# Decay tables of two chunked recurrences: ScalarE with a per-head bias in place of a bf16 matmul

## The reference, cut to what matters

```python
G = jnp.cumsum(gc, axis=-1)                                # layer 0: 32 heads, chunks of 128
decay = jnp.where(causal, jnp.exp(G[..., :, None] - G[..., None, :]), 0.0)
y_intra = jnp.einsum('bhnij,bhnjd->bhnid', scores * decay, xc)
...
A_cum = jnp.cumsum(A_dt, axis=-1)                          # layer 1: 128 heads, chunks of 128
L = jnp.exp(_segsum(A_dt))                                 # exp(A_cum_i - A_cum_j) for i >= j
Y_diag = jnp.einsum('bzlhn,bzshn,bhzls,bzshp->bzlhp', Cc, Bc, L, xch)
```

## Time and profile before

| | |
|---|---|
| median of 3 runs | 2715.9 us (2715.47 to 2716.67) |
| the profiled execution | 2718.86 us |
| its span in the trace | 2717.1 us |
| PE busy, share of the span | 2567.2 us, 94% |
| DVE busy | 1867.5 us, 69% |
| POOL busy | 1431.7 us, 53% |
| ACT busy | 1364.3 us, 50% |
| DMA | 118.79 MB, mean 44 GB/s |

### The profile page before, as it was taken

The page is one execution under the profiler, slowest core; times in us unless marked ns, Lnnn a source line. Parts: engine busy times, 40 slices in busy tenths (PEclk is TensorE's granted clock), DMA queues, the critical chain, the costliest instruction groups (busy, mean ns, idle before and its releaser), DMA issues.

```text
span 2717.1 us, 58923 instructions
## 1 busy us (share of the span) xinstructions
PE 2567.2 (94%) x19678; PEld 2041.7 (75%) x19678; DVE 1867.5 (69%) x2720; ACT 1364.3 (50%) x2492; POOL 1431.7 (53%) x1404
## 2 busy tenths in 40 slices
PE   4999999999999669899999999999999999999989
PEld 3778787787787448677777777777777777777777
DVE  5675766766757668767777677577676677785874
ACT  3434434334334245655664665665566646656621
POOL 1654655556546110456656656476575566574720
PEclk8999999999999869999999999999999999999999
DMA  2010110110110014211111111101111111111011
GB/s 89 24 50 27 34 44 23 44 40 19 51 36 12 17 66 138 88 33 44 40 33 58 37 38 49 38 29 52 43 38 50 33 58 34 41 49 38 18 47 47
DMA packets 72632, 118.79 MB, mean 44 GB/s; under 512 B 10310, under 2 KB 22214, under 8 KB 72373
## 3 DMA queue, kind: packets, MB, share of 16 engines
q1 hardware_dynamic: 72388, 115.61, 13.0%
HBM read 102.92 MB, written 12.65 MB: 43 GB/s over the span
## 4 chain that ended last, share of the span: by engine, by line
PE 48%; issue 4%; DVE 4%; POOL 2%; ACT 2%; DVEq 0%; POOLq 0%; ACTq 0%
PE proj L218 10%; PE proj L220 10%; PE proj L219 10%; PE core_y L1403 5%; PE core_o L1409 2%; PE turned L252 2%; DVE mx_acc L1214 2%; PE turned L1430 2%; PE decay L1462 1%; PE mx_decay L1462 1%; POOL mx_acc L1663 1%; PE mx_decay L220 1%; PE mx_decay L218 1%; PE mx_decay L219 1%; POOL mx_th L1660 1%
## 5 line engine op out<-in xcount | busy, mean ns | idle before, releaser
L201 DVE TENSOR_TENSOR slab_lo<-slab_raw,slab_hi 128x512 fp32r<-128x512 f32 (+2 forms) x272 | 256.9, 957 | 147.4 <-ACT slab_hi L192 121.6
L218 PE MATMUL proj<-slab_hi,XTL 128*128 128x512 f32 x816 | 355.0, 435 | 0.0
L218 PE MATMUL proj<-XTH,slab_lo 128*128 128x512 f32 x736 | 300.0, 408 | 37.5 <-PEq L81 14.4
L220 PE MATMUL proj<-slab_hi,XTH 128*128 128x512 f32 x816 | 320.7, 393 | 0.0
L219 PE MATMUL proj<-slab_lo,XTH 128*128 128x512 f32 x816 | 318.5, 390 | 0.0
L220 PE MATMUL proj<-XTH,slab_hi 128*128 128x512 f32 x736 | 292.3, 397 | 0.0
L219 PE MATMUL proj<-XTL,slab_hi 128*128 128x512 f32 x736 | 292.0, 397 | 0.0
L1660 POOL TENSOR_TENSOR mx_th<-mx_th,mx_acc 128x512 f32<-128x512 f32 x48 | 62.1, 1294 | 369.0 <-ACT mx_th L1560 368.9
L1677 POOL TENSOR_TENSOR mx_gate<-mx_gate,mx_hd 128x512 f32<-128x512 f32 x128 | 171.1, 1336 | 156.4 <-DVE mx_hd L1591 145.4
L218 PE MATMUL proj<-slab_hi,mx_otl 128*128 128x512 f32 x576 | 241.9, 420 | 0.0
L220 PE MATMUL proj<-slab_hi,mx_oth 128*128 128x512 f32 x576 | 227.7, 395 | 0.0
(11 more groups left out here) (351 smaller groups left out, 6719.5 us busy)
## 6 DMA issues: line engine op xcount, KB each, us to landing
slab_raw<-in_w_gate SPq DMA_DIRECT2D x64, 256.0 KB, 3.0
slab_raw<-in_w_out SPq DMA_DIRECT2D x64, 256.0 KB, 3.0
slab_raw<-in_w_x SPq DMA_DIRECT2D x60, 256.0 KB, 3.6
slab_raw<-in_w_q SPq DMA_DIRECT2D x32, 256.0 KB, 3.0
slab_raw<-in_w_g SPq DMA_DIRECT2D x32, 256.0 KB, 3.0
slab_raw<-in_w_o SPq DMA_DIRECT2D x32, 256.0 KB, 2.9
bc_scratch<-bc_acc SPq DMA_DIRECT2D x32, 256.0 KB, 2.0
slab_raw<-in_w_bc SPq DMA_DIRECT2D x20, 256.0 KB, 4.5
```

The costliest lines, as they stand in the source:

```text
L201: op = nc.vector.tensor_tensor(K.SL[par][:, c, 0:width], K.RAW[c][:, 0:width], hi, ALU.subtract)
L218: nc.tensor.matmul(to[:, 0:bh.shape[-1]], al, bh, start=(c == 0), stop=False)
L220: mm = nc.tensor.matmul(to[:, 0:bh.shape[-1]], ah, bh, start=False, stop=(c == KC - 1))
```

## The change

No decay matmul is left. `decay_phase` stores only G, in fp32, one DMA, and turns G (and R) onto the token partitions as `upto` (and `left`, negated). SP then broadcasts rows of G from DRAM to all 128 partitions: in the attention four DMAs of 512 KB a round, in the mixer eight of 512 KB a half (runs of 512 B), the first four of them ahead of everything else in the mixer's first half. ACT subtracts and clamps in one Relu a head (four of 128x128 with a bias of one column in place of one of 128x512), then takes the same Exp. Across chunks four Exps a bank, with a bias, take the place of one. The fixed rows, their buffers and their memsets are gone, and DVE now waits for the score bank by itself.

```diff
-                nc.tensor.matmul(PS[k % 2][:, :], KH[:, js], QH[:, :, qs], start=False, stop=True)
-                pe.wait_ge(S["at_rows"], HEAD + 48 * (g + 1))
-                pe.wait_ge(S["at_e"], HEAD + PAIRS * g + k - 1)
-                nc.tensor.matmul(PD[k % 2][:, :], LHS[:, int(p == 1), jt * P:(jt + 1) * P], RHS[:, b, :, (it % 2) * P:(it % 2 + 1) * P],
-                                 start=True, stop=True).then_inc(S["at_pair"], 1)
+                nc.tensor.matmul(PS[k % 2][:, :], KH[:, js], QH[:, :, qs], start=False, stop=True).then_inc(S["at_pair"], 1)
...
-            act.wait_ge(S["at_set"], HEAD + 1)
+            act.wait_ge(S["at_ld"], HEAD + 48)
...
+                            act.wait_ge(S["at_rows"], HEAD + 64 * (g + 1))
                             act.wait_ge(S["at_m"], HEAD + PAIRS * g + k - 1)
+                            alone(act)
+                            for h in range(REP0):
+                                src, head = GB[b][:, h, it * P:(it + 1) * P], ds(REP0 * g + h, 1)
+                                if p == 1:
+                                    ex = nc.scalar.activation(EX[k % 2][:, h, :], src, ACT.Exp, bias=left[:, jt, head])
+                                else:
+                                    rl = nc.scalar.activation(EX[k % 2][:, h, :], src, ACT.Relu, bias=upto[:, jt, head], scale=-1.0)
...
-            nc.vector.memset(LHS[:, :, :], 0.0)
-            nc.vector.memset(RHS[:, :, :, :], 0.0).then_inc(S["at_zero"], 1)
...
+            def row_load(q, t):
+                sp.wait_ge(S["mx_e"], HEAD + 16 * q + 2 * t - 6)
+                sp.dma_start(GB[t % 4][:, :, :], sums[ds(HH1 * q, HH1), t * P:(t + 1) * P].unsqueeze(0)
+                             .broadcast_to([P, HH1, P])).then_inc(S[f"mx_row{t % 4}"], 16)
...
+            for t in range(4):
+                row_load(0, t)
...
-                    row_loads(q, 0)
-                    row_loads(q, 1)
                     slab(q, 2)
-                    row_loads(q, 2)
-                    row_loads(q, 3)
+                    for t in range(4, NT):
+                        row_load(q, t)
...
                         slab(q, 3)
+                        for t in range(4):
+                            row_load(q + 1, t)
...
-                            nc.tensor.matmul(PD[k][:, :], LHS[b % 2][:, k, cols], RHS[b % 2][:, 4 * k:4 * k + 4, cols],
-                                             start=True, stop=True).then_inc(S["mx_d"], 1)
...
+                        act.wait_ge(S[f"mx_row{t % 4}"], HEAD + 32 * q + 16 * (t // 4 + 1))
                         for k in range(2):
-                            act.wait_ge(S["mx_d"], HEAD + 16 * q + 2 * t + k + 1)
-                            nc.scalar.activation(PD[k][:, :], PD[k][:, :], ACT.Relu, scale=-1.0).then_inc(S["mx_rl"], 1)
+                            act.wait_ge(S["mx_m"], HEAD + 16 * q + 2 * t + k - 1)
+                            if t == 0 and k == 1:
+                                act.wait_ge(S["mx_tap"], HEAD + 3 * (NT * q + 5))
+                            alone(act)
+                            for h in range(4):
+                                rl = nc.scalar.activation(PD[k][:, h * P:(h + 1) * P], GB[t % 4][:, 4 * k + h, :], ACT.Relu,
+                                                          bias=upto[:, t, ds(HH1 * q + 4 * k + h, 1)], scale=-1.0)
+                            rl.then_inc(S["mx_rl"], 1)
```

More of the change, by code:

```diff
@@ L449, in tile_xt_lo, with decay_phase @@
                             K.XTH[:, :, cols].bitcast(F32), ALU.subtract).then_inc(K.S[f"xl_{v}"], 1)
-def decay_phase(nc, K, d, layer, rows, dtk, from_start, to_end, first, first_width):
+def decay_phase(nc, K, d, layer, sums, dtk, turned, first, first_width):
     S = K.S
@@ L465, in decay_phase @@
     z, e, w, dd, q, G, R = (sb(f"dt{n}", wide) for n in ("z", "e", "w", "d", "q", "G", "R"))
[L466 to L469, removed]
     Z = 1 + (2 if layer else NB)
     LN = Z + 2
[L473 to L477, removed]
+    DT_READY, G_READY, R_READY = 8, 10, 11
     ones = sb("ones", [P, P])
@@ L488, in _ @@
             sp.dma_start(K.CB[:, :], d["conv_b"]).then_inc(S["bc_ld"], 16)
-            sp.dma_start(stage[:, :], d["head_rows"].rearrange("p h n -> p (h n)")).then_inc(S["mx_rows"], 16)
         first_loads(K, sp, N + 1, first, first_width)
[L491 to L500, removed]
+        sp.wait_ge(vv, HEAD + G_READY)
+        sp.dma_start(sums if layer else sums.rearrange("b h t -> (b h) t"), G[:, :]).then_inc(st, 16)
         if not layer:
-            sp.wait_ge(st, HEAD + 16 * 9)
+            sp.wait_ge(st, HEAD + 16)
     @block.tensor
@@ L560, in _ @@
         nc.scalar.activation(R[:, :], dd[:, :], ACT.Exp, scale=-1.0).then_inc(av, 1)
[L561 to L572, removed]
@@ L624, in _, with attention_phase @@
         step(left)
[L625 to L629, removed]
     K.slab += 1
     K.unit += 2
-def attention_phase(nc, K, d, rows, dtk):
+def attention_phase(nc, K, d, sums, dtk, upto, left):
     S = K.S
@@ L679, in attention_phase @@
         K.OTL = [sb(f"otl{i}", [P, KC, P], F32R) for i in range(2)]
[L680 to L683, removed]
+        GB = [sb(f"g_all{b}", [P, REP0, SEQ]) for b in range(NB)]
         block = mem.enter_context(nc.Block())
@@ L1333, in mixer_phase @@
         K.OTL = [sb(f"otl{i}", [P, KC, P], F32R) for i in range(2)]
-        RHS, LHS = K.RHS, K.LHS
+        GB = [sb(f"g_all{i}", [P, HH1, P]) for i in range(4)]
         tri = sb("tri", [P, P])
@@ L1340, in mixer_phase @@
         block = mem.enter_context(nc.Block())
-        G3, N3 = rows
         def whole(ap):
@@ L1849, in layout @@
     cos, sin = np.cos(ang.astype(np.float64)), np.sin(ang.astype(np.float64))
-    head_rows = np.zeros((15, HH1, SEQ), np.float32)
-    for h in range(HH1):
-        for i in range(3):
-            head_rows[3 + 3 * (h % 4) + i, h] = -1.0
     return {
```

157 lines of the change are left out of this document (62 added, 95 removed).

## The result

The changed kernel takes 2708.3 us (median of 20 runs, 2691.0 to 2723.9) against 2716.4 for the kernel before on the same chips (20 runs, 2708.3 to 2724.2). The ratio is 0.997, with a 95% interval of 0.9957 to 0.9983: faster, clear of the noise, but by 8 us (0.3%) where the forecast had 41. The changed kernel's profiled execution took 2711.6 us, 7.3 less than that of before (2718.9).

What follows compares the result with a forecast made beforehand. PE was taken as the bound (688 of 700 us busy in the attention, 1371 of 1400 in the mixer). Terms -18 - 16 - 8 - 5 + 6.5 = -40.5 us gave 2675 us; 8-in-10 range 2645 to 2722.

Steps and rivals of the forecast that it cites:

- The mixer's halves: Mixer, 16 halves: 1.4 us lost at slot 10, 3.1 given back, 0.6 new waits each; -18 us (-56 to +26).
- Its part about ACT: Mixer banks on ACT: Relus start 0.30 us apart, 0.70 us more a bank, 179 us in the mixer.
- PE's part: Decay matmuls leaving PE at 0.22 us a bank: 56 us in the mixer, 21 us in the attention.
- they lie beside PE: Mixer after its start: broadcasts issued four tiles ahead stay hidden, adding 45 GB/s to 41.
- the rival of slow broadcasts: Mixer broadcasts move slowly: about 2690 us at 100 GB/s, near 2790 at 50 GB/s; chance 0.14.
- The mixer's start: Start of the mixer: four broadcasts queued ahead of the first gate chunk delay ACT's first split; +6.5 us (0 to +20).
- Ahead of the mixer: End of decay_phase 1: G and R are turned earlier, so PE goes on near 995.5; -5 us (-7 to -1).
- The attention: Attention rounds: ten banks' 0.22 us return, two banks' gain is lost waiting for POOL's xc; -16 us (-21 to -3).
- The first set-up: End of decay_phase 0: one store instead of nine and no row filling let the attention start earlier; -8 us (-10 to -3).
- ScalarE as the bound: Mixer rival: Relus start further apart than 0.30 us and ACT holds PE up; about 2719 us at 0.395; chance 0.19.
- The rival that ACT never holds PE up: Mixer rival: slot 10 does not slip and PE keeps its whole gain; about 2633 us; chance 0.09.
- What would show it: Signs listed beforehand: 352 fewer matmuls, 1056 more ACT instructions, slot 10 waits of 1.5 to 2 us, later first split.

Runs made afterwards that it cites:

- rows_both: The changed kernel with layer 1's sums stored for 4 KB runs and the first four mixer broadcasts queued behind the first gate weights; 2673.8 us.
- rows_both_memset: rows_both with POOL's memsets and casts of the kernel before put back into decay_phase 1, on buffers nobody reads; 2681.1 us.
- early_5_6: rows_both with ACT making the two decay banks of a half's first tile in slots 5 and 6 instead of both in slot 8; 2640.1 us.
- rows_behind_gate: The changed kernel with the mixer's first four broadcasts queued behind the first gate weights and mx_BT/mx_CT instead of ahead; 2692.7 us.
- rows_contiguous: The changed kernel with layer 1's sums stored as (tile, head, 128), so a mixer broadcast reads one 4 KB run per partition; 2681.7 us.
- rows_once: The changed kernel without any mixer broadcasts but the first four, later tiles using the first half's rows again; 2691.5 us.

## Why the prediction was wrong

The direction was right, in part by luck: the stages ahead of the mixer gave 47 us where 29 were forecast, and with the 29 the kernel would have come out some 10 us slower than before. Four of the steps were mis-sized.

**The mixer's halves, -18 forecast, +17.7 measured: the term that failed.** Its part about ACT was nearly right. The Relus were priced at 0.395 us and 0.30 apart and are 0.37 and 0.29; slot 10 was to slip by 1.40 beside the 0.17 of the earlier trace rows, and PE waits 1.48 and 1.93. PE's part was right as well: 53 us came back where 56 were forecast. Two things were missing. The first is the traffic: "they lie beside PE" was argued from bytes, 45 GB/s on 41, and the rival of slow broadcasts from landing times. What counted was the number of packets, through PE's instructions that came late, which no wait in the profile before hints at: 13.6 us of stops and 8.5 of clock behind them. With 4 KB runs the same bytes cost the halves 21.4 us less (+17.7 to -3.7). The second is the clock behind a wait of 1.9 us, which the sum put at nothing: 1.7 us in seven groups, 12 in all. The two come to 34 of the 35.7 us by which the term was off, as far as one execution of each kernel can tell. With the rows mended (rows_both) the halves still stood at -0.6 instead of -18. Six such stretches, 10 us, explain more than half of that, and the new waits for POOL's `mx_xch`, 7 us, about the rest, which is also what two executions can differ by.

**The mixer's start, +6.5 forecast, +21.2 measured**, just outside its bounds (0 to +20). The step named the right cause and sized it by 246 GB/s. Beside the 512 B runs the DMA engines moved less, above all in the first 10 us (the last two columns are DMA share and GB/s), and SP stood in its issues for 9.9 us, which the sum had as four short ones.

```profile
1053.00:1063.00 10.00, 10.00 (x40) 8.07 (x39) 0.00 (x0) 0.00 (x0) 0.00 (x0) 0.85 0.42 112
1063.00:1076.00 13.00, 2.17 (x10) 1.47 (x8) 0.00 (x0) 1.23 (x1) 0.00 (x0) 0.76 0.76 202
```

**Ahead of the mixer, -5 forecast, -15.8 measured.** The earlier turning of G gave what was forecast. The other 10 us are POOL's memsets and casts, which the prediction took for free, because nobody waits for them: with them put back (rows_both_memset) the same stretch gives -5.1 instead of the -15.0 of rows_both. They slowed DVE, and the row was in the trace: 7.71 us for four instructions that take 1.92.

**The attention, -20.8 for -16.** The 20.8 are 2.6 a round, 12 banks at 0.22: everything came back. The first two banks were to be lost in the wait for POOL's `xc`. That copy took 1.47 us before and takes 1.04 now, and PE's wait shrank to 0.77 instead of growing to 1.5. What stretched the copy before is not shown: DVE's weight split runs beside it in both traces (0.57 us of it before, all of it now), while the multiplication by the scores (L906, 0.68 us) ran beside it only before. The first set-up gave 10.3 for 8; in the other kernels, whose code is the same up to there, it gave between 7.1 and 10.8.

**Rivals.** ScalarE as the bound was to decide from 0.39 us on; the pitch was 0.29, and still ACT's place in the order cost some 35 us, by the wait and the clock behind it rather than by its load: early_5_6 gives ACT the same work as rows_both and is 30 us (by the ratios) to 34 us (by the medians) faster. That rival's own price was off: at 0.395 apart a bank is 3 x 0.395 + 0.43 + 0.49 = 2.10, so 1.96 more a tile, not 2.16. Nothing came to rest on it. The rival that ACT never holds PE up, 2633, is nearly what early_5_6 reaches. The slow broadcasts came true in part: landing in 8.9 us is 59 GB/s, near the 55 at which that rival turned slower, but it expected full queues and not stops of PE, and the DMA engines were busy for 0.36 of the mixer.

**What would show it.** 352 matmuls fewer: right (19326 for 19678). ACT has 1047 instructions more, where 1056 were forecast, and is 203 us more busy instead of 250. PE's waits at slot 10, 1.5 to 2 us in every half: right (1.48 and 1.93). ACT's first split of the mixer was to come 7 us later and came after 23.7 us of idling instead of 5.7.

## What to carry to other kernels

Work that leaves the busiest engine gives its time back only where its substitute does not stand in front of something that engine waits for; look at the order in the helper's queue before its load, and put the new work where it idles anyway. Lay out what a DMA will broadcast so that each partition reads one long run, and queue it behind what is needed first. A write that nobody waits for can still be on the path, if it slows the engine next to it.

## What was not expected of the hardware

- The length of a DMA's runs, at equal bytes: 512 B runs land in 8.9 us and hold the issuing queue up to 5.0 us, 4 KB runs in 3.7 and 0.43. The Trainium skill, DMA: Bandwidth & Descriptors, section Specifications, gives 512 B as enough for line rate; these broadcasts, at 59 GB/s from issue to landing, took 2.4 times as long as with 4 KB runs, so the trace differs.
- Beside such short packets PE stopped inside a run of matmuls for up to 5.1 us. In 11 of 12 stops of over 1 us it went on 1.2 to 1.6 us after a 16 KB packet of instructions had landed. Three of the places are the same matmuls in the change and in rows_behind_gate, others differ from execution to execution.
- In the six kernels with both of a half's first banks in slot 8 of ACT (the change, rows_behind_gate, rows_contiguous, rows_once, rows_both, rows_both_memset) a wait of 1.9 us was followed by 3.4 us at half clock in 32 of 48 places, one of 1.5 us in none of 48.
- A row of five memsets on POOL, two of them of 128x2048 bf16, stretched a DVE instruction of 0.54 us to 6.4.
- ACT's Relu of 128x128 with a bias and a column offset from a register starts every 0.29 us, DVE's subtract and min every 0.26.
